# A dot-product interaction model on one core: the last half's pairs computed in two passes, without packing for the second

## What is computed

```python
x = relu(dense @ Wb0 + bb0); x = relu(x @ Wb1 + bb1)
d = relu(x @ Wb2 + bb2)
sp = emb[arange(26)[None, :], sparse_idx]
T = concatenate([sp, d[:, None, :]], axis=1)          # 27 vectors
Z = einsum('bnd,bmd->bnm', T, T)
li, lj = np.tril_indices(27, -1)
h = concatenate([d, Z[:, li, lj]], axis=1)            # 64 + 351
h = relu(h @ Wt0 + bt0); h = relu(h @ Wt1 + bt1)
p = sigmoid(h @ Wt2 + bt2)
```

## Time and profile before

| | us |
|---|---|
| median of 3 runs | 521.64 |
| lowest, highest | 521.49, 522.31 |
| the profiled execution | 521.22 |
| its span, first to last instruction | 519.5 |
| POOL busy, PE busy, DVE busy in the span | 379.6, 312.4, 243.5 |
| last gather issued at | 504.33 |
| mean granted TensorE clock | 0.724 |

### The profile page before, as it was taken

How to read it: one execution, slowest core, us unless ns; L and a number is a source line. 1 busy time by engine, 2 the same in 40 slices (tenths; PEclk the granted TensorE clock), 3 DMA queues, 4 the chain that set the end, 5 groups by cost and what they waited for, 6 DMA issues and landing times.

```text
span 519.5 us, 12002 instructions
## 1 busy us (share of the span) xinstructions
PE 312.4 (60%) x3396; PEld 226.2 (44%) x3396; DVE 243.5 (47%) x372; ACT 14.0 (3%) x26; POOL 379.6 (73%) x406
## 2 busy tenths in 40 slices
PE   2899983784474455534455624545436283479797
PEld 1333431672372334523245522544326262377765
DVE  5433866593464335643258325562546343542212
ACT  1000000000000000000000000000000000012211
POOL 5777777777777777777777777777777777777760
PEclk9978977695576756757568665675667775589699
DMA  6444323333244433444334443344334544332320
GB/s 204 40 27 29 28 32 26 30 30 27 31 30 28 27 29 29 29 27 28 28 29 27 29 27 29 27 29 27 28 29 28 29 29 27 27 28 28 27 29 3
DMA packets 19961, 16.84 MB, mean 32 GB/s; under 512 B 11683, under 2 KB 12972, under 8 KB 19897
## 3 DMA queue, kind: packets, MB, share of 16 engines
q0 software_dynamic: 12800, 13.13, 32.2%
q1 hardware_dynamic: 4378, 2.68, 3.7%
q10 hardware_dynamic: 2732, 0.51, 2.6%
HBM read 16.28 MB, written 0.01 MB: 31 GB/s over the span
## 4 chain that ended last, share of the span: by engine, by line
POOL 63%; issue 21%; PE 10%; DMA 3%; DVE 2%; POOLq 0%; ACT 0%; DVEq 0%; ACTq 0%
POOL rows L356 63%; PE ps_t L400 3%; DMA rows<-in_emb,idx_row 2%; PE ps_turn L408 1%; PE ps_feat L391 1%; PE ps_feat L513 1%; PE ps_gram L391 1%; DVE vecs_mv L986 1%; DMA idx_raw<-in_idx 1%; PE ps_gram L503 1%; DVE hb L787 0%; PE ps_turn L422 0%; PE ps_t L586 0%; PE ps_t L538 0%; PE ps_feat L538 0%
## 5 line engine op out<-in xcount | busy, mean ns | idle before, releaser
L356 POOL DMA_INDIRECT rows<-in_emb,idx_row x392 | 370.4, 945 | 122.5 <-issue 118.7
L422 PE MATMUL ps_turn<-ident,rows 128*128 128x128 f32 x182 | 41.0, 366 | 142.6 <-DMA rows<-in_emb,idx_row 133.9
L829 DVE COPY vecs_st<-ps_turn 128x512 f32<-128x512 f32 (+1 forms) x49 | 47.0, 959 | 110.8 <-PE ps_turn L422 110.4
L829 DVE COPY vecs_mv<-ps_turn 64x512 f32<-64x512 f32 (+1 forms) x98 | 96.1, 981 | 0.7
L422 PEld LDWEIGHTS ps_turn<-ident,rows 128*128 128x128 f32 x182 | 26.8, 182 | 157.7 <-issue 148.5
L467 PE MATMUL ps_gram<-vecs_mv,vecs_st 128*32 128x54 f32 x1792 | 41.4, 274 | 27.8 <-DVE vecs_mv L829 14.8
L467 PEld LDWEIGHTS ps_gram<-vecs_mv,vecs_st 128*32 128x32 f32 x1792 | 37.5, 155 | 33.2 <-DVE vecs_mv L829 17.6
L586 PE MATMUL ps_t<-wt_sb,ht_t 128*128 128x256 f32 x128 | 51.4, 571 | 0.0
L586 PEld LDWEIGHTS ps_t<-wt_sb,ht_t 128*128 128x128 f32 x128 | 34.9, 286 | 15.1 <-issue 8.1
L854 DVE STREAM_TRANSPOSE gram_s<-ps_gram 128x864 f32<-128x864 f32 x16 | 17.3, 1083 | 45.4 <-PE ps_gram L467 36.3
L565 PE MATMUL ps_t<-feat_t,wt_sb 117*128 117x128 f32 x180 | 35.3, 351 | 0.2 <-ACT feat_t L722 0.2
(11 more groups left out here) (80 smaller groups left out, 244.4 us busy)
## 6 DMA issues: line engine op xcount, KB each, us to landing
fetched<-in_emb SPq DMA_DIRECT2D x1024, 0.2 KB
fetched<-in_emb ACTq DMA_DIRECT2D x1024, 0.2 KB
rows<-in_emb,idx_row POOLq DMA_INDIRECT x400, 3.6
wt_sb<-in_wt SPq DMA_DIRECT2D x1, 1024.0 KB
wb_sb<-in_wb SPq DMA_DIRECT2D x1, 512.0 KB
wt_sb<-in_wt SPq DMA_DIRECT2D x1, 512.0 KB
idx_raw<-in_idx SPq DMA_DIRECT2D x1, 179.0 KB, 2.8
wt_sb<-in_wt ACTq DMA_DIRECT2D x1, 128.0 KB
```

The costliest lines, as they stand in the source:

```text
L356: nc.gpsimd.indirect_dma_start(rows[:, t, h * DIM:(h + 1) * DIM], None, emb_rows, bass.IndirectOffsetOnAxis(idx_row[:, c:c + 1], 0)).then_ ...
L422: turned = nc.tensor.transpose(ps_turn[r % 2][:, j, :], rows[:, first + j, :], ident[:, :])
L829: moved = nc.vector.tensor_copy(to, source)
```

## The change

Only the second half of the last step changes. Its 27 vectors are stored in another order (`EARLY_VECS`): the 19 that land first, then the eight late tables. The pairs are made in two passes.

- **Early pass.** `gram_last(1)` makes the 19 by 19 products of all 128 samples in one run, after `turn_last(11)` and `turn_late(0)`. VectorE turns them (`turn_early`, 608 and 288 columns in place of 864 and 416), ScalarE packs 171 entries (`pack`), two transposes, one move, and eight matmuls (`top_0_early`, weights `wt0_early_sb`) add them onto the open sums of the first layer.
- **Late pass.** `gram_late(q)` makes, per sample, the products of all vectors with the eight late ones, 32 by 8. There is no packing: one VectorE transpose of 256 columns (`stand_late`) into `late_s`, two transposes on TensorE (`turn_late_feat`), one copy each on ScalarE and VectorE (`move_late`), and eight matmuls of 128 rows (`top_0_late`, weights `wt0_late_sb`, zero rows where a pair is counted elsewhere) finish the first layer. `turn_feat_last` now stands for the two early tiles.
- The matmuls of `top_0_d_last` stand ahead of `turn_last(11)`. `stay_busy` stands four times with one matmul each, in place of 13 matmuls.
- Two more weight loads of 512 KB each stand on SyncE's queue at the start, ahead of `wt1_sb`; the waits for the top weights count 7 loads in place of 5.

```diff
+EARLY = VECS - LATE_N
+EARLY_D = EARLY - 1
+EARLY_DELTAS = (EARLY - 1) // 2
+EARLY_PAIRS = EARLY_DELTAS * EARLY
+EARLY_TILES = [(0, (EARLY_PAIRS + 1) // 2), ((EARLY_PAIRS + 1) // 2, EARLY_PAIRS)]
+
+
+EARLY_VECS = list(range(LATE)) + list(range(LATE + LATE_N, VECS)) + list(range(LATE, LATE + LATE_N))
...
+            sp.dma_start(wt0_early_sb[:, :, :], wt0_early.rearrange("k p n -> p k n")).then_inc(top_loaded, 16)
+            sp.dma_start(wt0_late_sb[:, :, :], wt0_late.rearrange("k p n -> p k n")).then_inc(top_loaded, 16)
...
-            def gram_last():
+            def gram_last(h):
 
                 i = STEPS - 1
 
-                pe.wait_ge(vecs_act, (NR + 1) // 2)
-                pe.wait_ge(vecs_dve, i * NR + NR // 2)
-                pe.wait_ge(d_placed, STEPS)
+                done = (NR, LAST_NR)[h]
+                pe.wait_ge(vecs_act, (done + 1) // 2)
+                pe.wait_ge(vecs_dve, i * NR + done // 2)
+                if h == 0:
+                    pe.wait_ge(d_placed, STEPS)
+                else:
+
+                    pe.wait_ge(gram_turned, i * 4 + 2)
+                part = slice(DIM * h, DIM * (h + 1))
+                n = (VECS, EARLY)[h]
                 for u in range(2):
                     for g in range(HALF):
                         for v in range(4):
                             c = 64 * u + 16 * v + g
                             summed = nc.tensor.matmul(
-                                ps_gram[32 * v:32 * v + 32, u, g * VECS:(g + 1) * VECS],
-                                vecs_st[0:DIM, c, :], vecs_st[0:DIM, c, 0:VECS],
-                                start=True, stop=True, tile_position=(0, 32 * v))
+                                ps_gram[32 * v:32 * v + n, u, g * n:(g + 1) * n],
+                                vecs_st[part, c, 0:n], vecs_st[part, c, 0:n],
+                                start=True, stop=True, tile_position=(DIM * h, 32 * v))
                 summed.then_inc(gram_summed, 1)
 
-            def gram_quarter(q):
+            def gram_late(q):
 
                 if q == 0:
-                    pe.wait_ge(gram_turned, (STEPS - 1) * 4 + 2)
+                    pe.wait_ge(gram_turned, STEPS * 4)
 
                 done = LAST_NR + (q + 1 if q < QUARTERS - 1 else len(LATE_RUNS))
                 pe.wait_ge(vecs_act, (done + 1) // 2)
@@ -501,43 +555,34 @@
                     for v in range(4):
                         c = 64 * u + 16 * v + g
                         summed = nc.tensor.matmul(
-                            ps_gram[32 * v:32 * v + 32, u, g * VECS:(g + 1) * VECS],
-                            vecs_st[part, c, :], vecs_st[part, c, 0:VECS],
+                            ps_gram[32 * v:32 * v + 32, u, g * LATE_N:(g + 1) * LATE_N],
+                            vecs_st[part, c, :], vecs_st[part, c, EARLY:VECS],
                             start=True, stop=True, tile_position=(DIM, 32 * v))
-                if q == QUARTERS - 1:
-                    summed.then_inc(gram_summed, 1)
-
-            def stay_busy(n):
+                summed.then_inc(late_summed, 1)
...
+            def turn_late_feat():
+
+                pe.wait_ge(late_stood, 1)
+                for k in range(LATE_TILES):
+                    turned = nc.tensor.transpose(late_blocks[k], late_s[:, k, :], ident[:, :])
+                turned.then_inc(late_turned, 1)
+
+            def top_0_late(m):
+
+                if m == 0:
+                    pe.wait_ge(late_low, 1)
+                for k in range(LATE_TILES):
+                    if m == 0 and k == 1:
+                        pe.wait_ge(late_high, 1)
+                    summed = nc.tensor.matmul(top_0_blocks_last(m // 2)[:, m % 2, :],
+                                              wt0_late_sb[:, k, m * P:(m + 1) * P],
+                                              late_t[:, k, :], start=False, stop=(m % 2 == 1 and k == LATE_TILES - 1))
+                if m % 2 == 1:
...
+            def top_0_early(m):
+
+                if m == 0:
+                    pe.wait_ge(feat_moved, STEPS * 2)
+                for k, (lo, hi) in enumerate(EARLY_TILES):
+                    nc.tensor.matmul(top_0_blocks_last(m // 2)[:, m % 2, :], wt0_early_sb[0:hi - lo, k, m * P:(m + 1) * P],
+                                     feat_t[0:hi - lo, 1, k, :], start=False, stop=False)
+
+            def turn_feat_last():
+
+                pe.wait_ge(feat_packed, STEPS * 2)
+                for k, (lo, hi) in enumerate(EARLY_TILES):
+                    turned = nc.tensor.transpose(ps_feat[1][0:hi - lo, k, :], feat[:, 1, lo:hi], ident[:, :])
+                turned.then_inc(feat_turned, 1)
...
                 top_1_sum(i, 0)
+                for m in range(T0 // P):
+                    top_0_d_last(m)
                 turn_last(11)
                 top_1_bias(i, 1)
+                turn_late(0)
+                gram_last(1)
+                stay_busy(1)
+                turn_late(1)
+                stay_busy(1)
+                gram_late(0)
+                gram_late(1)
+                turn_feat_last()
+                turn_late(2)
+                top_0_early(0)
+                top_0_early(1)
+                gram_late(2)
+                top_0_early(2)
+                turn_late(3)
+                turn_late(4)
+                top_0_early(3)
+                gram_late(3)
+                stay_busy(1)
+                turn_late_feat()
+                stay_busy(1, ps_gram[:, 1, 0:T1])
                 for m in range(T0 // P):
-                    top_0_d_last(m)
-                for q in range(QUARTERS):
-                    turn_late(q)
-                    if q == QUARTERS - 1:
-                        turn_late(q + 1)
-                    stay_busy((2, 2, 2, 1)[q])
-                    gram_quarter(q)
-                    stay_busy((0, 1, 1, 4)[q])
-                turn_feat_last()
-
-                pe.wait_ge(feat_moved, STEPS * 2)
-                for k in range(PAIR_TILES - 1):
-                    for m in range(T0 // P):
-                        top_0_last(k, m)
-                pe.wait_ge(last_tile_moved, 1)
-                for m in range(T0 // P):
-                    top_0_last(PAIR_TILES - 1, m)
+                    top_0_late(m)
                 top_1_sum(i, 1)
...
+            def stand_late():
+
+                dve.wait_ge(late_summed, QUARTERS)
+                products = ps_gram[:, :, 0:HALF * LATE_N].rearrange("p b (c v) -> p v b c", v=LATE_N)
+                nc.vector.transpose(late_s[:, :, :].rearrange("p k c -> p (k c)"), products).then_inc(late_stood, 1)
+
+            def move_late():
+                dve.wait_ge(late_turned, 1)
+                nc.vector.tensor_copy(late_t[:, 1, :], late_blocks[1]).then_inc(late_high, 1)
...
+            def turn_early():
+
+                dve.wait_ge(gram_summed, STEPS * 2)
+                nc.vector.transpose(gram_s[1][:, 0:EARLY * SLOTS], early_products(EARLY)).then_inc(gram_turned, 1)
+
+                nc.vector.transpose(gram_s[1][:, EARLY * SLOTS:(EARLY + EARLY_DELTAS) * SLOTS], early_products(EARLY_DELTAS))\
                     .then_inc(gram_turned, 1)
...
                 spread_late(0)
+                pack(i, 1)
+                move_feat(i, 1)
                 spread_late(2)
                 spread_late(4)
-                pack_last()
-                move_feat_last()
+                move_late()
...
                 spread_last(11)
+                turn_early()
                 spread_late(1)
                 spread_late(3)
-                turn_gram(i, 1)
-                pack_last()
-                move_feat_last()
+                stand_late()
+                move_late()
```

109 lines of the change are left out of this document (58 added, 51 removed).

## The result

The changed kernel takes 528.10 us (median of 10 runs, 523.77 to 532.51), the kernel before 522.43 beside it (521.29 to 524.03). One of its ten runs, 532.51, counts as disturbed and is left out of what follows. The ratio of runs side by side is 1.0089, 95% interval 1.0072 to 1.0107: about 4.6 us slower, 526.3 on the scale of the forecast of 525.0. The profiled execution took 527.79, its span is 526.0.

What follows compares the result with a forecast made beforehand. The prediction took 400 serial gather issues as the bound up to the last gather, then TensorE's list after the change. Terms -3.15 + 3.4 + 0.6 + 2.7 = +3.55 on 521.22 gave 524.8, adjusted to 525.0; range 519.9 to 527.6.

Steps and rivals of the forecast that it cites:

- The sign: Whole kernel: the change makes it slower, above 522.7 us, with chance 0.58.
- the mechanism: In `gram_last(1)`: the unbroken run of 256 small records is stopped waiting for code, taking 5.2 us rather than 2.8.
- the two causes: In TensorE's tail: late instruction code stops the run, and the granted clock falls to half behind it.
- Start cost 0: Kernel start: two more weight loads on SyncE's queue, 2 x 0.57 us, fit its 1.4 us idle; cost 0, bound 0.3.
- Start of `gram_last(1)`: TensorE's early run was to start at 499.55, with the `top_0_d_last` matmuls filling idle time ahead of 497.61.
- Term 2: Work ahead of the last products: they end later, +3.4 us, with `gram_last(1)` at 5.2 us; +1.0 with 2.8.
- Term 3: A second code stop at the next block border, in `gram_late(0)`: +0.6 us, between 0 and 1.3.
- Term 4: Behind the early run: TensorE's clock falls to half and comes back late, +2.7 us, bounds 0 and 6.
- Term 1: From the last products to the second layer: 3.1 us in place of 6.25, so -3.15 us.
- Rival 1: TensorE's tail: code arrives in time and the clock stays up, giving 519.5 us; chance 0.18.
- The end of the gathers: Before the change, the chain was read as going through the last gather, issued at 504.33 and landing at 506.7.

Runs made afterwards that it cites:

- b2: The kernel before with two unneeded 256-column matmuls right behind its `gram_last`, the first half's run of products; ratio to the kernel before 1.0012.
- e3: The changed kernel with ten more 27-column products, 40 instructions, ahead of `turn_last(11)`; one execution, 847.21 us, where the kernel before took 837.1.
- e5: The changed kernel with the early products of `gram_last(1)` replaced by 12 matmuls of 128 columns; ratio to the kernel before 1.0053.
- e1: The changed kernel with three unneeded 256-column matmuls inside `gram_last(1)`, run where the kernel before took 837.1 us; ratio to the kernel before 1.0097.
- e7: The changed kernel with both early and late products replaced by wide matmuls of the same TensorE time; ratio to the kernel before 1.0005.
- e9: The changed kernel with three unneeded 256-column matmuls inside `gram_last(1)` and three inside the first half's run `gram_last(0)`; ratio to the kernel before 1.0116.
- e6: The changed kernel with the products of each `gram_late` replaced by 3 matmuls of 128 columns; ratio to the kernel before 1.0055.
- e2: The changed kernel with four unneeded 256-column matmuls in place of one behind `gram_last(1)`, run where the kernel before took 837.1 us; ratio to it 1.0075.
- e8: The changed kernel with three unneeded 256-column matmuls inside `gram_last(1)`, the same kernel as e1, in the ordinary condition; ratio to the kernel before 1.0108.
- e10: The changed kernel with seven single `stay_busy` inside `gram_last(1)`, two behind it and one in each late quarter; ratio to the kernel before 1.0135.
- b1: The kernel before without its 13 `stay_busy` matmuls in the quarters, run where the kernel before took 837.1 us; ratio to it 1.0014.

## Why the prediction was right, and where it was not

The sign, the mechanism and the two causes were right, and the ratio's 526.3 lies 1.3 us from the forecast. Part of that closeness is luck: the sum itself was 3.0 us too low on the two profiled executions, which lie further apart than the runs do on average. By its steps, on the profiled execution:

- **Start cost 0: right, but not for the reason given.** The two loads were to fit into 1.4 us of idling; the late weights' load alone took 2.62 us to issue, and the queue's fetches begin at 10.50 where they began at 8.15. The gathers did not wait for them: the last one is issued 0.17 us later than in the earlier trace rows.
- **Start of `gram_last(1)`, 499.55:** 500.00 here, 501.7 to 504.3 in other executions. This is the step that failed. The prediction counted the `top_0_d_last` matmuls at nothing, since they fill the 1.14 us of waiting ahead of 497.61. Here the list reached them at 497.34, 0.9 later than in the earlier trace rows, as the first half's run began 0.9 later, and of their 0.89 us 0.62 came through at `turn_last(11)`. A cover was counted as free that covers upstream delays too, and only one trace of it was read. It is worth 1.1 to 1.3 us; the rest of a start at 504.3 is the delay itself, and what the order before makes of the same delay was seen in one execution only, b2's.
- **Term 2, a run of 5.2 us with a stop:** 5.4, stop 1.8, at the counted border. The choice between 2.8 and 5.6 was decided rightly by the row of the same kind. The Trainium skill, "Runtime: NRT & Kernel Launch", section "Instruction fetch mechanics", has the block of 256 instructions that e3 shows; that crossing its border is mostly hidden does not hold for the unbroken runs of 256 small records here: each has one or two stops of 0.7 to 2.5 us, though some borders pass without one, as that behind record 119 of the first half's run in the changed kernel.
- **Term 3, +0.6 for a second stop:** none is to be seen in the changed kernel, whose late products run at half clock; at full clock it shows, 0.48 in e5 and 0.92 in e1. Right as a mechanism, and swallowed by term 4.
- **Term 4, +2.7 (bounds 0 and 6):** under-sized. Terms 3 and 4 together were 3.3; the comparison with e7 gives 5.0 behind the run. The last products, forecast to end at 514 at half clock, end at 517.25. The forecast gave half the clock to the wide records up to a third of `top_0_late`. It also slowed the narrow late products (128 in 1.89 us, where e5 took 1.45), and it lasted until 519.7.
- **Term 1, −3.15:** right where the clock is up. In e5 the last products end at 513.24 and the second layer starts at 516.50, 3.26 us; forecast 3.1. In the changed kernel itself it is 4.1 (517.25 to 521.38), because of the clock.
- **Rival 1** (no stop, clock up, 519.5, faster): e7 is its experiment, and is 1.0005, not 0.996. Its way, 13.7, is 0.7 over what the sum gives for it (499.55 to 512.6), and its start is 4.3 us later than the changed kernel's, of which the lost wait for a gather explains 1.1 to 1.3. So even without code stops of its own the new order was not shown to be faster, though its fastest runs were.
- **The end of the gathers.** The prediction took the last gather, at 504.33, for what sets the end before the change. The chain of before leaves the gathers at 494.35. No term of the sum rests on this, since all were taken from stamps.

The sum was 3.55 and the profiled difference 6.57, 3.0 more: 0.45 from the start, 0.2 from the run, and 2.4 behind it. Of these 2.4, by e7, 0.7 is a list that is longer than counted (10.9 against 10.2 at full clock) and 1.7 the clock. How start and way are spread over the executions without a profile is not known.

## What to carry to other kernels

When work is moved ahead of the last arrival, ask first whether the engine that takes it had been waiting there, and for how long in a bad execution, not only in the one profiled: such a wait absorbs upstream stalls (1.3 us of them in b2). A long run of small fp32 products can eat code faster than it arrives, so count its instructions and break the run with work that is needed anyway. A few wide matmuls behind or inside such a run can bring back more clock than they cost (3 us of the way, net, for three calls), twelve brought nothing. And a stretch read from one profile is one draw: here it differed by 2.7 us between two kernels with the same code in it.

## What the runs showed of the hardware

- TensorE's code is used in blocks of 256 instructions, and a border can be placed to the record: 40 instructions ahead moved the stop by 20 records of two instructions each. Stops at borders took 0.3 to 2.5 us, ended 2.3 to 2.9 us after the start of an instruction packet, and varied between executions of one kernel (1.16 against 1.70 + 1.69). A border can also pass without a stop (behind record 119 of the first half's run in the changed kernel; that whole run in e9, with wide matmuls in it).
- The clock fell to 1.2 GHz 2.7 us into the early run and came back 17 us later in the changed kernel, but 3.4 us after its fall when wide matmuls stood in place of the late products (e6), and 3.4 us after it with four wide matmuls behind the run (e2). Three wide matmuls inside the run delayed the fall to 517 (e8); with three in either half's run it came at 512 (e9). With twelve calls it did not fall (e10). Why e8 and e9 differ is open.
- Small products in four column groups: 64 records in 0.70 us at full clock, 11 ns each. The Trainium skill, "TensorE: Matmul & The Clock Gate", section "Wait — 56ns, not 53.3ns?", puts a floor of about 25 ns on the distance of matmuls; the measured row decides.
- The kernel before took 522 us and 837 us in two conditions. In the slow one the chain of b1 lies for 40% of the span on SyncE's issuing of the small direct fetches (L327), which is not on the page's chain before. Why they were slow there stays open.
